# The experts' input and output turned by VectorE in squares of 32 and carried through DRAM, where TensorE turned them

## What is computed

```python
# x2: tokens x 128, after a layer norm and a modulation per sample
scores = sigmoid(x2 @ gate_w.T)                 # 16 experts in 4 groups
# best 2 groups by the sum of their two best scores, best 4 experts in them,
# their scores normalised and times 2.5: combine[token, expert]
for e in range(16):                             # up 128 -> 64, down 64 -> 128
    routed += combine[:, e] * (relu2(x2 @ up_w[e].T) @ down_w[e].T)
shared = relu2(x2 @ shared_up.T) @ shared_down.T    # 128 -> 256 -> 128
out = routed + shared                           # times a gate per sample, added to x
```

## Time and profile before

| | us |
|---|---|
| median of 3 runs (2126.47 to 2128.8) | 2126.95 |
| time of the profiled execution | 2126.03 |
| its span in the trace | 2124.1 |
| busy: PE, DVE, ACT, POOL | 2019.2, 1648.8, 1433.4, 615.6 |
| experts stage, first transposes to last measuring | about 1003 to 1332 |
| one run of the experts, from one to the next | 18.96 |

### The profile page before, as it was taken

The page is one execution under the profiler, slowest core; times in us unless marked ns, Lnnn a source line. Parts: engine busy times, 40 slices in busy tenths (PEclk is TensorE's granted clock), DMA queues, the critical chain, the costliest instruction groups (busy, mean ns, idle before and its releaser), DMA issues. The chain is left out here.

```text
span 2124.1 us, 40168 instructions
## 1 busy us (share of the span) xinstructions
PE 2019.2 (95%) x14693; PEld 1356.0 (64%) x14693; DVE 1648.8 (78%) x3999; ACT 1433.4 (67%) x1915; POOL 615.6 (29%) x859
## 2 busy tenths in 40 slices
PE   2899999999999999997899999799999996999998
PEld 1577777777777777776444444577777773444443
DVE  3888988888988888873666775577777766999997
ACT  1688777888777888774577776566666663555554
POOL 1344444544444544443000000233333330000000
PEclk9899999999999999997899999899999997999999
DMA  6000000000000000001564553000000000000000
GB/s 167 21 21 20 12 21 21 21 21 21 11 21 21 21 21 21 12 21 31 135 131 106 107 121 81 1 2 2 2 2 2 2 2 1 11 16 11 16 11 20
DMA packets 55361, 69.37 MB, mean 33 GB/s; under 512 B 13008, under 2 KB 32640, under 8 KB 55168
## 3 DMA queue, kind: packets, MB, share of 16 engines
q1 hardware_dynamic: 55168, 66.82, 13.4%
HBM read 45.30 MB, written 4.72 MB: 24 GB/s over the span
## 5 line engine op out<-in xcount | busy, mean ns | idle before, releaser
L864 POOL TENSOR_SCALAR_AFFINE_SELECT pr<-pr 128x512 f32<-128x512 f32 x256 | 202.4, 814 | 371.1 <-ACT pr L795 371.1
L422 PE MATMUL a_pO<-va,pr 128*128 128x66 f32 x2048 | 303.1, 271 | 1.9 <-POOL pr L864 1.5
L422 PEld LDWEIGHTS a_pO<-va,pr 128*128 128x128 f32 x2048 | 272.0, 192 | 18.9 <-issue 15.4
L1614 ACT ACTIVATE c_pr<-c_pS 128x1536 f32<-128x1536 f32 x128 | 186.0, 1453 | 119.2 <-PE c_pS L1426 119.2
L1669 POOL TENSOR_SCALAR_AFFINE_SELECT c_pr<-c_pr 128x512 f32<-128x512 f32 x256 | 158.4, 643 | 264.8 <-DVE c_pr L1534 264.8
L761 ACT ACTIVATE sq<-a_pW 128x512 f32<-128x512 f32 x192 | 114.4, 597 | 148.5 <-PE a_pW L363 145.8
L789 ACT ACTIVATE th<-a_pS 128x1536 f32<-128x1536 f32 x128 | 186.0, 1453 | 30.1 <-PE a_pS L407 29.6
L423 PE MATMUL a_pO<-va,pr 128*128 128x66 f32 x1024 | 198.2, 275 | 0.0
L795 ACT ACTIVATE pr<-th 128x1536 f32<-128x1536 f32 x128 | 190.5, 1489 | 3.1
L407 PE MATMUL a_pS<-qs,k 128*128 128x512 f16 (+1 forms) x1024 | 187.3, 326 | 0.9 <-issue 0.9
L1534 DVE TENSOR_SCALAR c_pr<-c_pr 128x1536 f32<-128x1536 f32 x128 | 122.6, 958 | 78.4 <-ACT c_pr L1614 78.4
(11 more groups left out here) (245 smaller groups left out, 4425.1 us busy)
## 6 DMA issues: line engine op xcount, KB each, us to landing
b_cwB<-b_by_expert SPq DMA_DIRECT2D x64, 512.0 KB, 8.5
k<-k SPq DMA_DIRECT2D x64, 256.0 KB, 3.6
x<-in_L_attn_tokens_dram SPq DMA_DIRECT2D x8, 512.0 KB, 7.1
out_dram<-x SPq DMA_DIRECT2D x16, 256.0 KB, 2.3
d_h<-in_L_ffn_h_w_dram SPq DMA_DIRECT2D x2, 1024.0 KB, 7.7
b_by_expert<-b_cwT SPq DMA_DIRECT2D x64, 8.0 KB, 1.8
wmod<-in_L_wmod_dram SPq DMA_DIRECT2D x2, 384.0 KB, 4.1
d_w<-in_L_ffn_w_w_dram SPq DMA_DIRECT2D x3, 256.0 KB, 3.2
```

Source lines behind the costliest of these rows:

```text
L422: pe.matmul(out, w[:, hh * N + t * P:hh * N + (t + 1) * P], v[:, 0, p, :], start=True, stop=t == 0)
L864: last = gp.affine_select(out=part, in_=part, compare_op=ALU.is_ge, fill=0.0, base=0, pattern=[[0, HPG], [1, P]], channel_multiplier=-1)
L1614: act.activation(pr[g][:, :, :], pS[:, :, 0:N + P], ACT.Exp, scale=float(1.0 / np.sqrt(np.float32(DQ)))).then_inc(s_ex, 1)
```

## The change

PE's eight transposes of each run go, with the PSUM banks `pX` and `pB`. Instead:

- **Input.** DVE normalises into `xn`, laid out in groups of 32 features, and turns it in one instruction in squares of 32x32 into `xt`. SP stores `xt` with four DMAs into DRAM, with pieces of 512 bytes and 64 KB each (`sp_put_in`), waits for them, and reads the block back with one DMA of 256 KB into `xh` (`sp_get_in`), features on the partitions. `act_modulate` reads `xh`. The normalising of run n+3 now stands in DVE's iteration n behind pair 4, and runs 0 and 1 are turned ahead of the loop.
- **Output.** ACT's gate writes `og` in the new layout, DVE turns it in one instruction into `ot` between pairs 3 and 4 (`dve_turn_out`), SP stores it with four DMAs (`sp_put_out`) and reads it back with one (`sp_get_out`) into `out`. DVE's adding of run n-1 moves from behind pair 4 to behind pair 8, with all of the measuring right behind it.
- **SP's order** in an iteration: small weight DMAs of n+1, `put_out` of n-1, weight loads of n+1, `get_out` of n-1, `put_in` and `get_in` of n+3. The in-trips of runs 0 and 1 stand ahead of the MLP's loads.

The diff, cut to its core:

```diff
+        S4 = P // SQ
+        xn, xt, xh, og, ot, out = (sb(x, [P, S4, T4, SQ]) for x in ('xn', 'xt', 'xh', 'og', 'ot', 'out'))
...
+        x_turned, out_turned = (nc.dram_tensor('b_' + x, (S4, SQ, S4, T4 * SQ), F32, kind='Internal').ap() for x in ('x_turned', 'out_turned'))
...
+        def sp_put_in(sp, n):
+            sp.wait_ge(s_xt, n + 1)
+            if n >= 1:
+                sp.wait_ge(s_xh, 16 * n)
+            for j in range(S4):
+                sp.dma_start(x_turned[:, :, j, :].rearrange('g s c -> s g c'), xt[SQ * j:SQ * (j + 1), :, :, :].rearrange('s g t r -> s g (t r)')).then_inc(s_xd, 16)
+        def sp_get_in(sp, n):
+            sp.wait_ge(s_xd, 16 * S4 * (n + 1))
+            if n >= 1:
+                sp.wait_ge(s_hT, n)
+            sp.dma_start(xh[:, :, :, :].rearrange('p j t r -> p (j t r)'), x_turned.rearrange('g s j c -> (g s) (j c)')).then_inc(s_xh, 16)
+        def sp_put_out(sp, n):
+            sp.wait_ge(s_ot, n + 1)
+            if n >= 1:
+                sp.wait_ge(s_out, 16 * n)
+            for g in range(S4):
+                sp.dma_start(out_turned[:, :, g, :].rearrange('j r c -> r j c'), ot[SQ * g:SQ * (g + 1), :, :, :].rearrange('r j t s -> r j (t s)')).then_inc(s_od, 16)
+        def sp_get_out(sp, n):
+            sp.wait_ge(s_od, 16 * S4 * (n + 1))
+            if n >= 1:
+                sp.wait_ge(s_st, ADD_STEPS * (n - 1) + 1)
+            sp.dma_start(out[:, :, :, :].rearrange('p g t s -> p (g t s)'), out_turned.rearrange('j r g c -> (j r) (g c)')).then_inc(s_out, 16)
...
         @block.sync
         def _(sp):
+            for n in range(2):
+                sp_put_in(sp, n)
+                sp_get_in(sp, n)
             ahead(sp)
...
+            for n in range(-1, RUNS + 1):
+                if 0 <= n + 1 < RUNS:
+                    sp_put_weights(sp, n + 1)
+                if 0 <= n - 1 < RUNS:
+                    sp_put_out(sp, n - 1)
+                if 0 <= n + 1 < RUNS:
+                    sp_get_weights(sp, n + 1)
+                if 0 <= n - 1 < RUNS:
+                    sp_get_out(sp, n - 1)
+                if 2 <= n + 3 < RUNS:
+                    sp_put_in(sp, n + 3)
+                    sp_get_in(sp, n + 3)
...
-                if 0 <= n + 2 < RUNS:
-                    pe_front(pe, n + 2)
...
-                if 0 <= n - 1 < RUNS:
-                    pe_back(pe, n - 1)
...
         def dve_normalise(dve, n):
...
+            dve.transpose(xt[:, :, :, :].rearrange('p g t r -> p (g t r)'), xn[:, :, :, :].rearrange('p g t s -> p (g t s)')).then_inc(s_xt, 1)
...
+        def dve_turn_out(dve, n):
+            dve.wait_ge(s_og, n + 1)
+            if n >= 1:
+                dve.wait_ge(s_od, 16 * S4 * n)
+            dve.transpose(ot[:, :, :, :].rearrange('p j t s -> p (j t s)'), og[:, :, :, :].rearrange('p j t r -> p (j t r)')).then_inc(s_ot, 1)
...
         def dve_add(dve, n):
-            dve.wait_ge(s_oT, n + 1)
-            add_to_x(dve, c, s_st, n, T4, pB[:, :])
+            dve.wait_ge(s_out, 16 * (n + 1))
+            xt4 = c.x[:, n * T4:(n + 1) * T4, :].rearrange('p t (g s) -> p t g s', s=SQ)
+            dve.tensor_tensor(xt4, xt4, out[:, :, :, :].rearrange('p g t s -> p t g s'), ALU.add).then_inc(s_st, 1)
...
                 if 0 <= n < RUNS:
                     dve_weigh(dve, n, 2)
                     dve_weigh(dve, n, 3)
+                if 0 <= n - 1 < RUNS:
+                    dve_turn_out(dve, n - 1)
+                if 0 <= n < RUNS:
                     dve_weigh(dve, n, 4)
-                if 0 <= n - 1 < RUNS:
-                    dve_add(dve, n - 1)
+                if 2 <= n + 3 < RUNS:
+                    dve_normalise(dve, n + 3)
...
                 if 0 <= n < RUNS:
                     dve_weigh(dve, n, 8)
                 if 0 <= n - 1 < RUNS:
+                    dve_add(dve, n - 1)
+                    dve_measure(dve, n - 1, 1)
+                    dve_measure(dve, n - 1, 2)
                     dve_measure(dve, n - 1, 3)
                 if 0 <= n + 2 < RUNS:
                     dve_chosen(dve, n + 2)
```

More of the change, by code:

```diff
@@ L944, in moe @@
         S2 = 2
+        SQ = 32
         RUNS = B // S2
@@ new lines, in sp_put_weights, with sp_get_weights @@
+        def sp_put_weights(sp, n):
+            sp.wait_ge(s_cT, n + 1)
+            if n >= 1:
+                for part in s_cw:
+                    sp.wait_ge(part, 2 * 16 * n)
+            for j in range(S4):
+                sp.dma_start(by_expert[:, :, j, :], cwT[SQ * j:SQ * j + E, :, :]).then_inc(s_cd, 16)
+        def sp_get_weights(sp, n):
+            sp.wait_ge(s_cd, 16 * S4 * (n + 1))
+            if n >= 2:
+                sp.wait_ge(s_a, RT * (n - 1))
+            rows = by_expert.rearrange('(k j y) t g r -> k y j (t g r)', k=2, y=2)
+            for k in range(2):
+                for y in range(2):
+                    sp.dma_start(cwB[n % 2][EI * y:EI * (y + 1), RT // 2 * k:RT // 2 * (k + 1), :],
+                                 rows[k, y].unsqueeze(0).broadcast_to((EI, RT // 2, W))).then_inc(s_cw[k], 16)
@@ L1007, in weights_of @@
         def weights_of(u):
             return RT + u if u < ST else u - ST
[L1010 to L1016, removed]
         def pe_route(pe, n):
@@ L1042, in pe_down @@
             pe.matmul(pD[:, :], dT[:, t * D:(t + 1) * D], a[(IT * n + u) % 4][:, :], start=u == 0, stop=u == IT - 1).then_inc(s_dn, 1)
[L1044 to L1050, removed]
         @block.tensor
@@ L1098, in dve_normalise @@
             if n >= 1:
-                dve.wait_ge(s_xT, n)
+                dve.wait_ge(s_xt, n)
             for t in range(T4):
-                last = normalise(dve, c, xn[:, t, :], n * T4 + t)
+                i = n * T4 + t
+                last = dve.tensor_scalar(xn[:, :, t, :], c.x[:, i, :].rearrange('p (g s) -> p g s', s=SQ), c.mv[:, i, 0:1],
+                                         c.rs[:, i:i + 1], ALU.subtract, ALU.mult)
             last.then_inc(s_xn, 1)
+            dve.wait_ge(s_xn, n + 1)
+            if n >= 1:
+                dve.wait_ge(s_xd, 16 * S4 * n)
+            dve.transpose(xt[:, :, :, :].rearrange('p g t r -> p (g t r)'), xn[:, :, :, :].rearrange('p g t s -> p (g t s)')).then_inc(s_xt, 1)
         def dve_scores(dve, n):
@@ L1197, in _ @@
             dve.wait_ge(s_km, 4)
+            dve_normalise(dve, 0)
+            dve_normalise(dve, 1)
             for n in range(-2, RUNS + 1):
@@ L1241, in act_modulate @@
                 act.wait_ge(s_up, IT * (n - 2))
-            act.wait_ge(s_xT, n + 1)
+            act.wait_ge(s_xh, 16 * (n + 1))
             for m in range(S2):
-                last = act.activation(hT[n % 3][:, m * N:(m + 1) * N], pX[:, m * N:(m + 1) * N], ACT.Identity, scale=c.mod[:, 0, 4, n * S2 + m:n * S2 + m + 1], bias=c.mod[:, 0, 3, n * S2 + m:n * S2 + m + 1])
+                last = act.activation(hT[n % 3][:, m * N:(m + 1) * N].rearrange('p (t j r) -> p t j r', t=TT, j=S4), xh[:, :, m * TT:(m + 1) * TT, :].rearrange('p j t r -> p t j r'), ACT.Identity, scale=c.mod[:, 0, 4, n * S2 + m:n * S2 + m + 1], bias=c.mod[:, 0, 3, n * S2 + m:n * S2 + m + 1])
             last.then_inc(s_hT, 1)
@@ L1271, in act_gate @@
             if n >= 1:
-                act.wait_ge(s_oT, n)
+                act.wait_ge(s_ot, n)
             act.wait_ge(s_dn, IT * (n + 1))
             for m in range(S2):
-                last = act.activation(og[:, m * N:(m + 1) * N], pD[:, m * N:(m + 1) * N], ACT.Copy, scale=c.mod[:, 0, 5, n * S2 + m:n * S2 + m + 1])
+                last = act.activation(og[:, :, m * TT:(m + 1) * TT, :].rearrange('p j t r -> p t j r'), pD[:, m * N:(m + 1) * N].rearrange('p (t j r) -> p t j r', t=TT, j=S4), ACT.Copy, scale=c.mod[:, 0, 5, n * S2 + m:n * S2 + m + 1])
             last.then_inc(s_og, 1)
```

41 lines of the change are left out of this document (7 added, 34 removed).

## The result

| | before | changed |
|---|---|---|
| median, us (of 3 and of 4 executions) | 2126.95 | 2256.12 |
| lowest to highest | 2126.47 to 2128.8 | 2253.93 to 2257.36 |
| span of the profiled execution | 2124.1 | 2255.6 |
| mean granted PE clock in it | 0.978 | 0.956 |

The ratio is 1.0606, 95% interval [1.0591, 1.0621]: 129 us slower. Forecast were 2281 (+154), with 2215 to 2330 as the range.

A forecast was written before the change was run, and what follows sets the result against it. PE was taken to bound the kernel before, and a loop through SP's DMA queue the changed one. Loop +125, start +21 and end +8 gave +154 us on the median 2126.95, so 2281, with 2215 to 2330 as the range.

The forecast's parts named there:

- The loop: Steady passes of the experts: one output's block transpose to the next takes 27.8 us against 18.84 before; 14 intervals, +125 us.
- `put_out` to the output's return: SP's queue: four stores issued, weight loads landing 12.5 us after first issue, then the read's data 1.25; 16.4 us.
- adding, measuring, choice, pair 9: DVE's work after the output returns, before PE can end the pass: 2.2, 0.9 and 0.7, together 3.8 us.
- last down at the lower clock: PE's last down product of a pass, after standing idle: 2.45 us at the lower clock, 1.55 at the upper.
- gate to the next `put_out`: ACT's gate through DVE's pair 3, 4.45 us, then the output's block transpose, 0.7 us.
- The clock: PE stands still 7 to 8 us in each loop, which supports the lower clock, 1.2 GHz, behind it.
- The start: Start of the experts stage: first input trips, MLP loads and first weights delay PE's route by 19.1, products add 1.8; +21 us.
- The end: End of the experts stage: the last output's trip adds 6.5 us and adding ahead of pair 9 adds 1.5; +8 us.
- Removed: PE's eight transposes a pass, 0.88 us, go; a pass bound by PE alone would take 18.1 us.
- Reads that overtake: Rival, chance 0.09: the output's read lands ahead of earlier loads' data, PE stays the bound, only the ends cost; 2146 us.
- The second wait on the input: Rival, chance 0.08: the input's read back comes 2 us late 14 times, 28 us more; 2310 us.
- The faster rival: Rival, chance 0.04: PE's freed 0.88 us in 16 passes, 14 us, is kept and trips lie beside other work; 2116 us.

The follow-up runs named there:

- the place of `get_out` in the queue: Changed kernel with the output's read back issued ahead of the next weight loads: 2204.91 us against 2256.12.
- the data ahead of it: Changed kernel with half of the expert weight loads left out after the first two passes of the experts, omitting part of the computation: 2166.9 us.
- what DVE has queued behind the wait: Changed kernel with DVE's adding and measuring moved from behind pair 8 to the next iteration's start, behind the expert weights: 2188.98 us.
- output only: Only the output's half of the change, with the input turned by PE as in the kernel before: 2251.39 us, ratio 1.0589 to the kernel before.
- run 2: Not a follow-up: the third of the 16 passes of the experts inside one kernel execution, counted from zero; no time of its own is given.
- run 0: Not a follow-up: the first of the 16 passes of the experts inside one kernel execution; no time of its own is given.
- the kernel that has no trips at the ends: Changed kernel with both trips before weight loads, two DRAM weight buffers, two PSUM sum banks, PE turning the first three inputs and last output: 2114.32 us.
- A second queue: Changed kernel with all put and get DMAs issued by GpSimd instead of SP: 2222.64 us, one execution of 9298 us left out.

## Why the prediction was right

**The loop: right.** The two traces, and four runs that each touch the loop at another place, agree: the place of `get_out` in the queue (-51 us), the data ahead of it (-89), what DVE has queued behind the wait (-67), and the half that contains the loop (output only, +125). In the order of the prediction, with the mean over the 14 intervals:

| step of the loop | forecast, us | measured, us |
|---|---|---|
| `put_out` to the output's return | 16.4 | 15.3 |
| adding, measuring, choice, pair 9 | 3.8 | 3.7 |
| last down at the lower clock | 2.45 | 2.2 |
| gate to the next `put_out` | 5.15 | 4.9 |
| sum | 27.8 | 26.06 |

The forecast of +125 us for the loop became 1441.43 - 1076.64 = 364.8 less 263.8, +101. That is 24 of the 25 us by which the prediction was too high. Two thirds of them, 16 us, are the first term, where I had written "Four small DMAs take 2.5 us to issue": that is the price of the small weight DMAs (L1022, still 2.50), but those of `put_out` take 1.76 in most runs, 0.44 each, and the first weight load leaves 1.9 us behind the first of them. The rest of that term is the data of `get_out`: the read lands 0.6 us behind the last load and not 1.25. The other 8 us are small errors of the same sign in the other three. PE also stands still for less than forecast: 5.7 us each time, and at most 7.0, not 7 to 8.

**The clock: right.** The windows view of the changed kernel behind such a gap:

```profile
1247.50:1253.50 6.00, 0.00 (x0) 0.00 (x0) 3.65 (x24) 0.58 (x1) 0.00 (x0) 0.87 0.52 126
1253.50:1257.50 4.00, 3.97 (x5) 1.80 (x6) 1.62 (x7) 1.51 (x4) 0.00 (x0) 0.50 0.04 5
```

Six us with no product, then 4 us at 0.50, thus 1.2 GHz.

**The start: right in size, in part by luck.** Forecast +21. The first `put_out` is 1076.64 - 1005.73 = 70.9 us into the stage; the same point lay at 1051.54 + 0.69 + 0.71 - 1002.64 = 50.3: +20.6. But two errors cancel in it. The route of run 2 comes 47.6 us into the stage and came 30.7 into it before: +16.9 where +19.1 was forecast, since the trips and the loads were shorter than their sum. From there to the first `put_out` it takes 3.7 us more and not 1.8. The weight loads of run 0 ahead of run 2's input, which the prediction had, are the larger cause. "Only now come the ten loads of the MLP" is a smaller one, of some 4 us, and it is not their place behind the trips that costs it, since ahead of them they hold up the trip of run 0 by as much.

**The end: right.** Forecast +8, measured (1467.15 - 1441.43) - (1335.72 - 1315.31 - 1.40) = 25.7 - 19.0 = +6.7. Sum: 101 + 20.6 + 6.7 = 128.3.

**Removed: half wrong.** "So a run bound by PE alone would take 18.1 us." It takes 18.5: without the input's transposes PE meets ACT's gate, 0.4 us a run. In the changed kernel this is hidden by the loop, so it cost the prediction nothing.

**The rivals.** Reads that overtake: fell, 10.4 us behind the loads, 2.6 without. The prediction said that no run shows a later transfer of the queue landing first. The changed kernel does show it, though only just: the first store of `put_in`, issued at 1160.56 behind the read at 1159.67, landed at 1170.0, and the read at 1171.3. In the 12 runs that have both, the store landed up to 1.3 us ahead of the read. That is far from the 8 us that this rival needed.

The estimate by the Trainium skill, "DMA: Bandwidth & Descriptors", "Anatomy of one DMA" (436 GB/s, given for DMAs issued by GpSimd; some 2193 us for the kernel) is not met by these loads of SP's: the four weight loads still land 12.4 to 13.9 us behind the first issue.

The second wait on the input: it had 4.6 us to spare, and came up as soon as the output's loop was opened. The faster rival needed the trips to cost nothing at both ends too; they do cost there, and only the kernel that has no trips at the ends, and three more changes in between, gains 12 of the 14 us named.

## What to carry to other kernels

Cost a small transfer by what its queue has ahead of it at that moment, not by its size: the same 256 KB took 2.6 or 10.4 us. Then write down what the engine that waits for it has queued behind the wait, and follow that on to the transfer's own next start. If the path comes back to where it began, a run can't be shorter than the way round, however idle the engines are. When an instruction is taken off the engine that is the bound, look for a wait that it covered.

## What was not expected of the hardware

- Four DMAs of different kinds take SP 1.76 us or 2.50 us to issue: the stores of 64 KB in pieces of 512 bytes 0.44 each, the weight DMAs of 8 KB in pieces of 128 bytes 0.62 each. Which of the differences makes it no run isolates, and the queue matters as well: the same four stores of 64 KB take 1.75 us with nothing ahead of them and up to 2.71 behind the weight loads, and the single read of 256 KB takes 0.34, or 0.66 behind them.
- A second queue did not help the stores past the loads: 7.5 us against 1.8. Yet they landed ahead of the last load, which was issued before them.
- The block transpose of 128x512 f32 takes 0.70 to 0.71 us, the one of 128x128 0.31. If the time grows evenly with the columns, some 0.18 us of it is fixed, an estimate from these two sizes.
